# Difference of the scores and the addition of both terms to the mix on VectorE instead of GpSimd, in the logic attention of a five-stage network

## The reference, cut to what matters

```
A1 = softmax(S1); A2 = softmax(S2)
Cr = log(A1 @ A2 + EPS); Cl = log(A2 @ A1 + EPS)
feat = stack([S1, S2, S1.T, S2.T, Cr, Cl])
gates = sigmoid(conv2(gelu(conv1(feat))))        # g_and, g_or, g_not, g_chain
Smix = S1 + g_and * S2 + g_or * (logaddexp(S1, S2) - S1) - g_not * (0.5 * S2) + g_chain * Cr
A = softmax(Smix)
y = A @ v1 + w * (A1 @ (A2 @ v2))
```

## Time and profile before

| | us |
|---|---|
| three runs, median | 2741.39 (2739.67 to 2742.15) |
| profiled execution, its own time | 2749.36 |
| its span | 2747.4 |
| periods of the logic attention with `z` and `m` both at work (`p` from 1 to 28) | 28 |
| length of one of them | 34.86 |

### The profile page before, as it was taken

One profiled execution on the slowest core, in us unless ns is written; L12 is line 12 of the kernel. 1 busy time (PEld: TensorE's weight loads), 2 busy tenths in 40 slices (PEclk: granted clock), 3 DMA queues, 4 the chain that ended last, 5 costly groups with the idle time before them and its releaser, 6 DMA issues. The chain is left out here.

```text
span 2747.4 us, 57727 instructions
## 1 busy us (share of the span) xinstructions
PE 2331.1 (85%) x22902; PEld 1654.3 (60%) x22902; DVE 1899.0 (69%) x2795; ACT 1681.4 (61%) x2553; POOL 570.3 (21%) x263
## 2 busy tenths in 40 slices
PE   5258999999999999998449994877838999999998
PEld 2145444444444444443137773766538999999998
DVE  0544888888888888886543335566368888887887
ACT  0036888888888888887514442333127777777776
POOL 0022444444444444442100001033000000000000
PEclk9658999999999999999659996789959999999999
DMA  4017777777777777777110000000022221222120
GB/s 163 0 58 208 208 216 215 216 213 212 212 214 216 215 206 212 212 210 186 28 46 1 0 0 8 2 1 3 20 75 91 73 79 65 66 72 79 65 73 32
DMA packets 110108, 307.04 MB, mean 112 GB/s; under 512 B 20220, under 2 KB 56822, under 8 KB 108967
## 3 DMA queue, kind: packets, MB, share of 16 engines
q1 hardware_dynamic: 109863, 303.62, 37.8%
HBM read 170.60 MB, written 80.65 MB: 91 GB/s over the span
## 5 line engine op out<-in xcount | busy, mean ns | idle before, releaser
L578 ACT ACTIVATE la_hid<-ps,la_b 128x904 f32<-128x904 f32 (+1 forms) x480 | 450.8, 989 | 68.7 <-PE ps L433 67.9
L1417 PE MATMUL ps<-ls_xm,ls_w_in_parts 128*128 128x226 f16 x3072 | 467.5, 261 | 12.7 <-DVE ls_xm L1498 8.3
L1425 PE MATMUL ps<-ls_state_parts,ls_w_rec_parts 128*128 128x226 f16 x2976 | 448.0, 259 | 0.0
L1444 ACT ACTIVATE ls_gates<-ps,ls_bias 128x226 f32<-128x226 f32 x768 | 301.5, 446 | 127.1 <-PE ps L1425 127.0
L433 PE MATMUL ps<-la_pairs,la_w 32*64 32x452 f32 x3584 | 309.2, 567 | 45.8 <-ACT la_hid L578 42.9
L1417 PEld LDWEIGHTS ps<-ls_xm,ls_w_in_parts 128*128 128x128 f16 x3072 | 294.4, 97 | 22.5 <-issue 8.7
L1425 PEld LDWEIGHTS ps<-ls_state_parts,ls_w_rec_parts 128*128 128x128 f16 x2976 | 285.2, 96 | 6.3
L446 PE MATMUL ps<-la_hid,la_w 128*32 128x452 f32 x1856 | 246.9, 556 | 1.0 <-ACT la_opened L584 1.0
L407 POOL TENSOR_TENSOR la_P<-la_S,la_top 113x904 f32<-113x904 f32 x64 | 153.3, 2395 | 263.9 <-DVE la_top L681 263.9
L433 PEld LDWEIGHTS ps<-la_pairs,la_w 32*64 32x64 f32 x3584 | 74.1, 130 | 185.9 <-issue 111.8
L584 ACT ACTIVATE la_opened<-ps,la_b 128x904 f32<-128x904 f32 x128 | 130.0, 1015 | 71.2 <-PE ps L446 60.0
(11 more groups left out here) (284 smaller groups left out, 4489.1 us busy)
## 6 DMA issues: line engine op xcount, KB each, us to landing
la_pairs<-la_maps SPq DMA_DIRECT2D x224, 452.0 KB, 6.1
la_gate<-la_opened SPq DMA_DIRECT2D x448, 113.0 KB, 4.1
ls_w_all<-ls_weights SPq DMA_DIRECT2D x32, 904.0 KB, 4.2
la_maps<-la_ST SPq DMA_DIRECT2D x32, 791.0 KB
la_maps<-la_S SPq DMA_DIRECT2D x32, 791.0 KB
ls_m_all<-ls_masks SPq DMA_DIRECT2D x32, 456.0 KB, 3.6
la_maps<-la_Cr SPq DMA_DIRECT2D x32, 395.5 KB
la_maps<-la_Cl SPq DMA_DIRECT2D x32, 395.5 KB
```

The source lines that it names most:

```text
L578: act.activation(hid[:, u % 4, 0:n], ps[:, bank:bank + n, 0:HALF], ACT.Gelu_apprx_tanh, bias=b1[:])\
L1417: mm = pe.matmul(out_j, w_in_parts[:, w, e, j, :], xm[:, t % 2, e, :, x, 0:N], start=((w, x) == PASSES[0]), stop=(t == 0 and (w, x) == PAS ...
L1425: mm = pe.matmul(out_j, w_rec_parts[:, w, e, j, :], state_parts[:, x, e], start=False, stop=((w, x) == PASSES[-1]))
L1444: return act.activation(dst, ps[:, n % 3 * 2 + j // 2, j % 2 * 256:j % 2 * 256 + C], ACT.Tanh if j == 3 else ACT.Sigmoid, bias=bias[:, e, ...
```

## The change

Both operations leave POOL's program and are made by DVE. The difference stands directly ahead of the absolute value in `absolute`; the addition of `Cr` stands in `mix_sum` as a second `tensor_tensor`, between the addition of `soft` and the row maxima, and adds `Cr` to the mix rather than to `soft`. The semaphore `two_terms` is gone, DVE makes `diff_ready` itself, and POOL waits for neither `soft_ready` nor `mix_step` any more.

```diff
-                    if ok(c):
-                        after(pool, s["soft_ready"], c)
-                        pool.tensor_tensor(diff[:], S[:, c % 4, 1], S[:, c % 4, 0], ALU.subtract).then_inc(s["diff_ready"], 1)
-                    if ok(m):
-                        pool.wait_ge(s["mix_step"], 5 * m + 3)
-                        pool.tensor_tensor(soft[:], soft[:], Cr[:, m % 3], ALU.add).then_inc(s["two_terms"], 1)
...
                 def mix_sum(m):
                     A = mix[:, m % 2]
-                    dve.wait_ge(s["two_terms"], m + 1)
                     dve.wait_ge(s["mix_step"], 5 * m + 5)
-                    signal(dve, dve.tensor_tensor(A, A, soft[:], ALU.add), s["mix_top_step"], 2 * m + 1)
+                    signal(dve, dve.tensor_tensor(A, A, soft[:], ALU.add), s["mix_top_step"], 3 * m + 1)
+                    signal(dve, dve.tensor_tensor(A, A, Cr[:, m % 3], ALU.add), s["mix_top_step"], 3 * m + 2)
                     dve.tensor_reduce(mix_top[:], by_head(A), AX_X, ALU.max).then_inc(s["mix_top_step"], 1)
...
                 def mix_shift(m):
                     A = by_head(mix[:, m % 2])
-                    dve.wait_ge(s["mix_top_step"], 2 * m + 2)
+                    dve.wait_ge(s["mix_top_step"], 3 * m + 3)
...
                 def absolute(c):
-                    dve.wait_ge(s["diff_ready"], c + 1)
+                    after(dve, s["soft_ready"], c)
+                    signal(dve, dve.tensor_tensor(diff[:], S[:, c % 4, 1], S[:, c % 4, 0], ALU.subtract), s["diff_ready"], c + 1)
                     dve.scalar_tensor_tensor(soft[:], diff[:], -1.0, diff[:], ALU.mult, ALU.max).then_inc(s["abs_ready"], 1)
```

More of the change, by code:

```diff
@@ L270, in logic_attention @@
                  "T_made T_ready chain_made ych_step ych_ready ET_made ET_ready base_made y_step yT_ready out_made added "
-                 "P_raised sum_step inv_ready P_ready mix_step gates_used two_terms mix_top_step mixed E_raised E_step "
+                 "P_raised sum_step inv_ready P_ready mix_step gates_used mix_top_step mixed E_raised E_step "
                  "E_inv E_ready diff_ready abs_ready abs_raised soft_logged soft_ready").split()
@@ L389, in _ @@
                 for p in PERIODS:
-                    m, c, f, z = p - 1, p, p + 2, p + 3
+                    m, f, z = p - 1, p + 2, p + 3
                     if ok(f):
```

## The result

The changed kernel takes **2814.18 us** (median of 4 runs, 2812.39 to 2815.87) against 2741.77 us for the kernel before (2739.67 to 2742.55): a ratio of 1.0256, 95% interval 1.0231 to 1.0282. I had forecast 2752.8 us with a range of 2738 to 2764. The direction was right, the size was wrong: +72 us came where I had +11. The profiled execution took 2815.87 us, its span is 2813.5, so 66.1 us more than the span before. Nearly all of it lies in the periods: from the second of the 32 ACT copies L596 (L590 now) to the 31st it is 1075.96 us against 1010.46, +65.5. This stretch holds 27 of the 28 late transports; the 28th comes behind the 31st copy.

The account below looks back on a forecast made before the run. The prediction took ACT, gapless with PE nearly back to back, to bound the period, and DVE to bound nothing. 28 x 0.5 = +14.0, less 1.85 and 0.75, gave +11.4 on 2741.4: 2752.8 us, range 2738 to 2764.

Parts of the forecast that it names:

- What bounds the period: Logic attention, 34.86 us period: ACT works without a gap, PE runs nearly back to back, DVE bounds nothing.
- DVE's lead of 1.88 us: At PE's transport: DVE delivers the values at 249.25 within 749.25, PE starts at 751.13, so 1.88 us early.
- POOL and DVE waiting for each other, who is queued first, 1.56 and 0.96 us: Two-input instructions: the later queued waits; POOL ends 1.56 us after DVE's, DVE's next 0.96 us after POOL's.
- The values 1.0 us late at the transport: DVE's values come at 752.08 instead of 749.25 (+2.83), so PE's transport starts 1.0 us late.
- Of this 0.55 is free ... first unit (half of the 1.01 us) is ready at 757.75 to 757.85: Behind the transport: 0.55 us absorbed; by the first convolution, GELU is +0.4 to +0.5 late; +0.5 us a period taken.
- The 0.55 us of `Cl`: ACT's `Cl` after PE's second product: 0.55 us to spare, so `Cl` would be late by 0.45.
- nothing absorbs the lateness: Rival: delayed first convolution also delays the second unit, using up ACT's 0.55; +25.4 us, 2767 us; chance 0.10.
- a period of 35.9: Sign of being wrong in the logic attention: 35.9 us periods, nothing absorbed, instead of 35.3 to 35.4.
- The drain: End of logic attention: DVE's earlier signal for gates gives -1.85 us, the last mix -0.75; together -2.6.
- The range: Whole kernel: 2738 to 2764 us, from hidden additions up to PE 0.4 later at the transport.
- The forecast's own case: Whole kernel: lateness partly absorbed, +0.5 us a period, 2752.8 us, between 2747 and 2764; chance 0.63.

Follow-up runs that it names:

- Two halves of the change: Kernel before with only the difference moved to DVE: 2745.66 us, ratio 0.9998; with only the addition of Cr moved: 2748.13 us, ratio 0.9989.
- late2: Kernel before plus two DVE reductions with unused results behind the absolute value; 2744.25 us, ratio 0.998.
- swap: Changed kernel with the addition ahead of the first row maxima and the difference ahead of the second on DVE; 2744.54 us, ratio 0.9986.
- fill1: Changed kernel plus one PE matmul with unused result ahead of the transport; 2777.44 us, ratio 1.0108.
- gap: Changed kernel with both added operations moved ahead of the first score copy, where DVE waits for PE; 2744.68 us, ratio 1.0001.
- fill2: Changed kernel plus two PE matmuls with unused results ahead of the transport; 2777.93 us, ratio 1.0115.
- late3: Kernel before plus three DVE reductions with unused results behind the absolute value; 2799.41 us, ratio 1.0186.
- late2h: Kernel before plus two DVE reductions and a third over 4 heads, results unused, behind the absolute value; 2748.85 us, ratio 1.0035.

## Why the prediction was wrong

- **What bounds the period, and DVE's lead of 1.88 us:** right. Two halves of the change and `late2` stay below it and cost nothing.
- **POOL and DVE waiting for each other, who is queued first, 1.56 and 0.96 us:** right, to 0.01 us over a replay of 15 us, and `swap` shows that the order of the two in the queue decides it.
- **The values 1.0 us late at the transport:** right (1.00).
- **"Of this 0.55 is free ... first unit (half of the 1.01 us) is ready at 757.75 to 757.85":** wrong. The term was mis-sized: the first GELU can start only 1.05 us after the first convolution begins, not 0.5. A convolution starting at 757.23 is ready at 758.28, 0.90 us after 757.38; the other 0.09 us is the weight load of the transport, for which the prediction had no term. So +0.99 a period, not +0.5: 14 us of the error. The row that says so was in the trace of before. Later in the period ACT waits for PE at the same kind of pair; PE starts it at 758.53, and ACT follows 1.05 later:

```profile
758.53 1.80 PE L433 MATMUL ps<-la_pairs,la_w 32*64 32x452 f32 x16 [0.77 <-ACT la_hid L578]
```

```profile
759.58 1.92 ACT L578 ACTIVATE la_hid<-ps,la_b 128x904 f32<-128x904 f32 x2 [0.28 <-PE ps L433]
```

  The 0.55 us of `Cl` was right by itself (`Cl` came 0.52 late), but it was not the way that ended last. The rival "nothing absorbs the lateness" (chance 0.10, +25.4) blamed the second unit where it was the first, and had the size of this part by luck; the prediction's own sign of being wrong, a period of 35.9, came true in the three periods at full clock.
- **A term was missing:** PE's clock. The sum put it at nothing without a reason: I counted PE's new standstill of 0.83 us as 0.83 us, and not that the matmuls behind it run at half the clock. 38 us of the error in the 27 periods up to the 31st copy, the largest part. A hint of it stands in the trace of before, where in a late period PE stands 3.66 us ahead of the first product, and everything behind is long (3.38 for 1.84, 1.73 for 0.96). It doesn't show that 0.83 us is enough:

```profile
1271.14 3.38 PE L486 MATMUL ps<-la_P,la_PT 113*113 113x113 f32 x16 [3.66 <-ACT la_PT L596]
1274.32 1.73 PE L495 MATMUL ps<-ident,la_mix 113*113 113x113 f32 x8
```

- **The drain:** forecast -2.6, not decided. From the copy L596 of the last full period to the next stage's first DVE instruction it was 132.4 us and is 131.4, and this stretch now contains the 28th late transport at a low clock (about +2.5 by the lengths above, an estimate). ACT's wait for gates there went from 5.53 to 4.19 us. But over the twelve traces the same stretch takes between 127.5 (`fill1`) and 135.8 us (`gap`), so none of these differences can be put down to the change.
- **The range:** no case in it held two independent costs of one late transport. The forecast's own case and the unabsorbed case would both have needed the clock's term on top.

What stays open: why three periods of after, and 22 of `fill1`, keep the clock while the others don't. With 0.83 us of standstill at the transport 25 of 28 periods fall, with 0.40 (`fill1`) 5 of 27, with none 0 of 27 (`fill2`); `late3` with about 0.5 falls in three periods of four. It isn't random within a trace: in after, from the second full period on, the fall starts 0.06 to 0.17 us later behind ACT's copy from one period to the next. Two of the three full-clock periods come right after it had reached 7.4 and 7.5 us, the third follows the one long stretch, and behind each the fall starts early again, at 5.8 to 6.1 us. No run shows what sets this.

## What to carry to other kernels

An operation moved between engines costs what lies after the last point at which the receiving engine waits anyway; here the time saved before that point was lost again in a wait, while behind it two instructions of 1.1 us, the added `+ Cr` and the old absolute value, became 2.5 each because another engine was queued first. Moving two instructions across a neighbour each (`swap`), or the two added ones into the wait (`gap`), took the whole cost away. And before a late arrival at a nearly full TensorE is priced at its length, look in the trace for matmuls that run long behind a standstill, and allow for that. Also read from the trace how long after a group of matmuls its consumer starts, instead of taking half of the group's length.

## What the runs showed of the hardware that was not expected

- Standstills of TensorE of 0.48 to 0.51 us (`late3`) and 0.83 us (after) once in a period of 37 us, beside one of 0.51 us that was there before, were in most periods followed by TensorE at 1.2 GHz for some 3.4 us; each such stretch cost 1.5 to 1.6 us. With 0.51 us alone (before, `late2`; `late2h` with 0.03 more) the clock stayed at 2.4 GHz in all full periods.
- Useless matmuls in the standstill made the kernel 37 us faster (2814 to 2777 us), with the transport as late as before.
- Two engines that wait for each other: POOL's subtraction ended 1.55 us after DVE's two-input instruction, and DVE's next one 0.96 us after that, twice in every period. With DVE's instruction queued ahead (`swap`) it took 1.09 us instead of 2.48.
- ACT could read the first half of 16 short matmuls only 1.05 us after their start, although the timeline has all 16 ending at 1.01: ends of matmuls in the timeline are modelled, and the consumer's start tells more.
